# Graph network kernel: the feed-forward part, three normalisations and the projection to relations as one staggered stage

## What is computed

```python
# third layer, after the attention sums
att_out = out.mean(axis=1) + bias_att
x1 = layer_norm(att_out + h, ln1_g, ln1_b)
ff = relu(x1 @ W1 + b1) @ W2 + b2            # 64 -> 128 -> 64
x = x + layer_norm(ff + x1, ln2_g, ln2_b)
# fourth layer
h = maximum(_layernorm(x), 0)
out = h @ W_self.T + b_self
for r in range(3):
    msg = msg + where(edge_type == r, h[src] @ W_rel[r].T, 0)
out = relu(out.at[dst].add(msg))
x = x + out
```

## Time and profile before

| | us |
|---|---|
| median of 3 runs (9044.34 to 9046.91) | 9044.35 |
| the profiled execution, own time | 9047.62 |
| its span | 9045.9 |
| node stage: first transfer issued to last DVE instruction | 6677.37 to 6833.18 |
| relation stage: to the first instruction of the edge pass | 6833.48 to 6925.52 |
| edge pass: to the start of the last PE stage | 6925.52 to 8961.2 |

### The profile page before, as it was taken

How to read it: one execution, slowest core, us unless ns; L and a number is a source line. 1 busy time by engine, 2 the same in 40 slices (tenths; PEclk the granted TensorE clock), 3 DMA queues, 4 the chain that set the end, 5 groups by cost and what they waited for, 6 DMA issues and landing times. The chain is left out here.

```text
span 9045.9 us, 111398 instructions
## 1 busy us (share of the span) xinstructions
PE 4987.4 (55%) x30696; PEld 3834.2 (42%) x30696; DVE 5704.2 (63%) x16144; ACT 2155.6 (24%) x3911; POOL 6276.7 (69%) x5705
## 2 busy tenths in 40 slices
PE   5888888888569999356666666666672000000000
PEld 3554454444358787345555555555561000000000
DVE  6888888888679999466666666666663222222222
ACT  0111111111035555034444444444420000000000
POOL 4888888888645555467777777777513777777776
PEclk9888888888779999555555555555555555555555
DMA  3333333333311111123333333333311222222221
GB/s 84 35 35 35 35 37 35 35 35 35 48 42 23 22 23 21 39 51 56 57 57 56 56 57 57 57 56 57 74 51 39 53 53 52 49 53 53 53 53 48
DMA packets 635687, 421.21 MB, mean 47 GB/s; under 512 B 533255, under 2 KB 542756, under 8 KB 632784
## 3 DMA queue, kind: packets, MB, share of 16 engines
q0 software_dynamic: 322560, 216.89, 20.2%
q1 hardware_dynamic: 310766, 197.07, 7.4%
q10 hardware_dynamic: 2304, 6.55, 0.2%
HBM read 234.91 MB, written 185.18 MB: 46 GB/s over the span
## 5 line engine op out<-in xcount | busy, mean ns | idle before, releaser
L1791 POOL DMA_INDIRECT rows_l<-att_row_table,slots_l x2016 | 2003.1, 994 | 647.2 <-issue 613.8
L892 POOL DMA_INDIRECT acc<-val,idx x1240 | 1919.8, 1548 | 417.8 <-issue 373.1
L1003 POOL DMA_INDIRECT rows_l<-relation_table,idx x1612 | 1529.2, 949 | 578.6 <-issue 491.0
L1014 DVE SCALAR_TENSOR_TENSOR run<-run,mask,rows_l 128x64 f32<-128x64 f32 x1612 | 459.7, 285 | 1571.7 <-DMA rows_l<-relation_table,idx 1516.2
L701 PE MATMUL banks<-part 128*128 128x490 bf16 (+1 forms) x5580 | 1295.3, 391 | 0.0
L1050 PE MATMUL banks<-run,link 128*128 128x64 f32 x98 | 21.1, 421 | 2039.9 <-PEq L983 2039.9
L1905 PE MATMUL banks<-rows_l,prob 128*128 128x65 f32 x4032 | 920.2, 420 | 45.1 <-ACT piece_part L1841 41.5
L1905 PEld LDWEIGHTS banks<-rows_l,prob 128*128 128x128 f32 x4032 | 879.0, 330 | 106.0 <-issue 86.6
L1152 POOL DMA_INDIRECT gathered_rows<-h_table,gathered_index x600 | 577.9, 963 | 446.8 <-ACT gathered_index L1262 272.8
L1050 PEld LDWEIGHTS banks<-run,link 128*128 128x128 f32 x98 | 21.0, 333 | 2040.6 <-issue 2040.6
L701 PEld LDWEIGHTS banks<-part 128*128 128x128 bf16 x5580 | 582.9, 107 | 637.4 <-issue 151.1
(11 more groups left out here) (383 smaller groups left out, 9206.3 us busy)
## 6 DMA issues: line engine op xcount, KB each, us to landing
piece_sums<-kept_l SPq DMA_DIRECT2D x252, 264.0 KB, 4.3
running_sums<-run SPq DMA_DIRECT2D x62, 832.0 KB, 3.5
attr<-in_edge_attr SPq DMA_DIRECT2D x61, 624.0 KB, 3.7
rows_l<-att_row_table,slots_l POOLq DMA_INDIRECT x2016
rows_l<-relation_table,idx POOLq DMA_INDIRECT x1612, 2.5
acc<-val,idx POOLq DMA_INDIRECT x1240, 3.2
gathered_rows<-h_table,gathered_index POOLq DMA_INDIRECT x600
acc<-zero ACTq DMA_DIRECT2D x12, 512.0 KB, 16.7
```

The lines of the kernel that those rows point to most:

```text
L892: e.indirect_dma_start(acc_d[k], bass.IndirectOffsetOnAxis(ap=idx[h][:, r:r + 1], axis=0), val[h][:, r, :], None, compute_op=ALU.add).then ...
L1003: e.indirect_dma_start(gbuf[h][:, r, :], None, table, bass.IndirectOffsetOnAxis(ap=idx[h][:, r:r + 1], axis=0))\
L1791: e.indirect_dma_start(rows[u][:, r, :], None, hx_d, bass.IndirectOffsetOnAxis(ap=slots[u][:, r:r + 1], axis=0))\
```

## The change

The node stage and the relation stage become one Block written out by hand. All work is cut into the seven parts (`span(c)`, 128x448 each), and the parts are staggered: in round t (0 to 9) the first normalisation handles part t, the feed-forward part on PE part t - 1, the second normalisation part t - 2, and the third normalisation's end, the transposes of h and the relation matmuls part t - 3. Differences in the work itself:

- `res` is loaded by seven transfers, one per part, instead of one; then `w3` and `b3` on the same queue.
- The subtraction of the mean is one `scalar_tensor_tensor` with the sum and -1/D; squares are taken by ACT (`squares`), the root by ACT with scale 1/D and an epsilon tile as bias; gains and shifts are `tensor_tensor` on POOL. The copies to `step` are gone: PE transposes straight from `x1` and `hs`.
- The row sums are prepared in the attention tail: DVE adds the attention bias row to `hs`, be2 to `xs`, and be1 to `bf2`, so that the stage has no instructions for them. Those two whole-tensor additions stand behind `src_i` in the DVE list.
- Relation results: ACT copies both the 192 relation columns and the 64 own columns, two nodes at a time, from three rotating PSUM banks; stores are three per part (128x448 each), 21 in place of 42.
- `link`'s iota goes to POOL's list after its last gain. The comparison for `link` and the bias addition to `own` (128x3136) go to the head of the edge pass's DVE list (`first(e)`).

The diff, cut to its core:

```diff
-        def edge_pass(name, table, index, gbuf):
+        def edge_pass(name, table, index, gbuf, first):
...
                     e.memset(run[1][:, HALF - 1, :], 0.0).then_inc(s_step, 1)
+                    first(e)
...
                     e.scalar_tensor_tensor(src_i[:, :], typ[:, :], float(NP), src_i[:, :], ALU.mult, ALU.add)
+                    e.wait_ge(s_par, 16 * 9)
+                    every = [P, J, D]
+                    e.tensor_tensor(hs[:, :, :], hs[:, :, :], bc(vecs["batt"][:, :].unsqueeze(1), every), ALU.add)
+                    e.tensor_tensor(xs[:, :, :], xs[:, :, :], bc(vecs["be2"][:, :].unsqueeze(1), every), ALU.add)
+                    e.tensor_tensor(vecs["bf2"][:, :], vecs["bf2"][:, :], vecs["be1"][:, :], ALU.add)
...
+                @block.gpsimd
...
+                    def att_gain(c):
+                        e.wait_ge(s_c1, 3 * c + 3)
+                        e.tensor_tensor(scaled[:, span(c), :], res[:, span(c), :], row(vecs["g1"]), ALU.mult)\
+                         .then_inc(s_g1, 1)
+                    def shift(c):
+                        e.wait_ge(s_n1, c + 1)
+                        e.tensor_tensor(x1[:, span(c), :], scaled[:, span(c), :], row(vecs["be1"]), ALU.add)\
+                         .then_inc(s_x1, 1)
+                        e.wait_ge(s_q1, c + 1)
+                        e.tensor_tensor(res[:, span(c), :], scaled[:, span(c), :], row(vecs["bf2"]), ALU.add)\
+                         .then_inc(s_xb, 1)
...
+                    for t in range(NCH + 2):
+                        if t < NCH:
+                            att_gain(t)
+                        if t >= 2:
+                            ffn_gain(t - 2)
+                        if t < NCH:
+                            shift(t)
+                    e.iota(link[:, :, :], [[1, J], [J, P]], base=0, channel_multiplier=0,
+                           allow_small_or_imprecise_dtypes=True)
...
+                    def x_scale(c):
+                        e.wait_ge(s_r3, c + 1)
+                        e.reciprocal(var[:, 2, span(c)], var[:, 2, span(c)]).then_inc(s_v3, 1)
+                        e.wait_ge(s_v3, 2 * c + 2)
+                        e.scalar_tensor_tensor(hs[:, span(c), :], hs[:, span(c), :], 0.0, per(var, 2, c), ALU.max,
+                                               ALU.mult).then_inc(s_h, 1)
...
+                    for t in range(NCH + 3):
+                        if t < NCH:
+                            att_centre(t)
+                        if t >= 3:
+                            x_variance(t - 3)
+                        if 2 <= t < NCH + 2:
+                            ffn_centre(t - 2)
+                        if t >= 3:
+                            x_scale(t - 3)
+                        if t < NCH:
+                            att_variance(t)
+                        if 2 <= t < NCH + 2:
+                            ffn_variance(t - 2)
+                        if t < NCH:
+                            att_scale(t)
+                        if 2 <= t < NCH + 2:
+                            ffn_scale(t - 2)
...
+                    for t in range(NCH + 3):
+                        if t < NCH:
+                            square(s_c1, 3 * t + 3, res, 0, t, s_q1, s_v1, 1)
+                        if t >= 3:
+                            root(s_v3, 2 * (t - 3) + 1, 2, t - 3, s_r3)
+                        if 1 <= t < NCH + 1:
+                            copy_x1(t - 1)
+                        if 2 <= t < NCH + 2:
+                            square(s_c2, 3 * (t - 2) + 3, res, 1, t - 2, s_q2, s_v2, 0)
+                        if t < NCH:
+                            root(s_v1, 2 * t + 2, 0, t, s_r1)
+                        if 2 <= t < NCH + 2:
+                            root(s_v2, 2 * (t - 2) + 1, 1, t - 2, s_r2)
+                        if 1 <= t < NCH + 1:
+                            relu(t - 1)
+                        if t >= 3:
+                            copy_h(t - 3)
+                            relations_out(t - 3, 0)
+                            relations_out(t - 3, 1)
+                        if 2 <= t < NCH + 2:
+                            square(s_c3, 3 * (t - 2) + 3, hs, 2, t - 2, s_q3, s_v3, 0)
+                        if t >= 3:
+                            relations_out(t - 3, 2)
+                            relations_out(t - 3, 3)
...
+                    e.wait_ge(s_w3, 32)
+                    for t in range(1, NCH + 3):
+                        if t < NCH + 1:
+                            turn_x1(t - 1)
+                            up(t - 1)
+                            down(t - 1)
+                        if t >= 3:
+                            turn_h(t - 3)
+                            for k in range(NR):
+                                relate(t - 3, k)
...
+            def before_rows(e):
+                e.tensor_scalar(link[:, :, :], link[:, :, :], linkf[:, 0:1], None, ALU.is_equal)
+                e.tensor_tensor(own[:, :, :], own[:, :, :], bc(b3_s[:, :].unsqueeze(1), [P, J, D]), ALU.add)
+            edge_pass("l3", y3_d, src_i, g, before_rows)
```

More of the change, by code:

```diff
@@ L1429, in build @@
         quads.close()
[L1431 to L1441, removed]
         att = ExitStack()
@@ L2199, in _ @@
                         last.then_inc(s_proj, 1)
[L2201 to L2243, removed]
+        relating = ExitStack()
+        own = sb("own", [P, J, D], f32, relating)
+        link = sb("link", [P, J, P], f32, relating)
+        b3_s = sb("b3", [P, D], f32, relating)
         with ExitStack() as ctx:
             w3_s = sb("w3", [D, 4 * D], f32, ctx)
[L2246 to L2251, removed]
[L2252 to L2295 removed]
@@ new lines, in build @@
+            res = sb("att_out", [P, J, D], f32, ctx)
+            scaled = sb("normed", [P, J, D], f32, ctx)
+            x1 = sb("x1", [P, J, D], f32, ctx)
+            eps = sb("layer_eps", [P, 1], f32, ctx)
+            sq = [sb(f"squares{n}", [P, JB, D], f32, ctx) for n in range(3)]
+            mean = sb("node_sums", [P, 3, J], f32, ctx)
+            var = sb("node_squares", [P, 3, J], f32, ctx)
+            xt = sb("x1_t", [D, JB * P], f32, ctx)
+            hid = sb("hidden2_t", [P, JB * P], f32, ctx)
@@ new lines, in build @@
+            ht = sb("h3_t", [D, JB * P], f32, ctx)
+            rel = [sb(f"relations{k}", [P, 3, JB, D], f32, ctx) for k in range(2)]
+            NCH = J // JB
+            PARTS = [(0, 4), (4, JB)]
+            ROUNDS3 = [(j, min(j + 2, JB)) for j in range(0, JB, 2)]
+            NR = len(ROUNDS3)
+            s_res = [sem(f"nodes_att_loaded{c}") for c in range(NCH)]
+            s_rel = [sem(f"relations_stored{k}") for k in range(2)]
+            (s_c1, s_q1, s_g1, s_r1, s_n1, s_x1, s_xb, s_xt, s_xc, s_up, s_hid, s_down, s_c2, s_q2, s_g2, s_r2, s_n2,
+             s_c3, s_q3, s_r3, s_h, s_ht, s_hc, s_mul, s_ev, s_w3, s_v1, s_v2, s_v3) = (sem(f"nodes_{n}") for n in (
+                "att_centred", "att_squared", "att_gained", "att_root", "att_scaled", "x1", "x1_and_bias", "x1_turned",
+                "x1_t_copied", "hidden", "hidden_relu", "ffn", "ffn_centred", "ffn_squared", "ffn_gained", "ffn_root",
+                "ffn_added", "x_centred", "x_squared", "x_root", "h", "h_turned", "h_t_copied", "relations",
+                "relations_copied", "weights", "att_variance", "ffn_variance", "x_variance"))
@@ L2297, in build @@
         with ExitStack() as ctx:
             g = [sb(f"rows_l3_{h}", [P, HALF, D], f32, ctx) for h in range(2)]
-            edge_pass("l3", y3_d, src_i, g)
+            def before_rows(e):
+                e.tensor_scalar(link[:, :, :], link[:, :, :], linkf[:, 0:1], None, ALU.is_equal)
+                e.tensor_tensor(own[:, :, :], own[:, :, :], bc(b3_s[:, :].unsqueeze(1), [P, J, D]), ALU.add)
+            edge_pass("l3", y3_d, src_i, g, before_rows)
         with ExitStack() as ctx:
@@ L2309, in build @@
             stage(ch)
+        relating.close()
+        late.close()
+        att.close()
 def kernel(**inputs):
```

202 lines of the change are left out of this document (162 added, 40 removed).

## The result

| | before | changed |
|---|---|---|
| median of 4 runs | 9044.35 us (9041.55 to 9046.91) | 8933.02 us (8932.81 to 8935.93) |
| profiled execution | 9047.62 | 8935.93, span 8934.2 |

The ratio is 0.9878, with a 95% interval of 0.9861 to 0.9895. The forecast of 8932 is 1 us off, but some of its terms are off by more. From first transfer (6675.75) to the first instruction of the edge pass (6809.95) the stage takes 134.20 us, where 248.15 stood before. The edge pass from there to the end of the span takes 8934.2 - 6809.95 = 2124.25, against 9045.9 - 6925.52 = 2120.38.

A forecast was written before the change was run, and what follows sets the result against it. PE, at 16.4 us per part, was taken to bound the new stage: 8.6 + 16.6 + 86.0 + 20.0 + 4.2 = 135.4 against 248.15, with 0.5 lost in the edge pass, giving 8932 us; range 8914 to 8958.

The forecast's parts named there:

- The bound: New stage: PE has the most work per part, 16.4 us against 10.6, 8.4 and 5.2; PE-bound stage, chance 0.70.
- I add 0.3 for relus that come late: Rounds 3 to 7: 0.3 us added to each round's 16.4 for PE waiting on late relus.
- 0.45 for the copy: Rounds 3 to 7: stall of 0.4 to 0.5 us each, as ScalarE evacuates, squares, roots, then copies the transpose.
- PE's 16.4: PE's work per part: 8.3 us for a feed-forward turn plus 8.1 for a relation turn.
- The same step, round 3: First of rounds 3 to 7, which hold feed-forward and relations: all five priced at 17.2 us, 86.0 together.
- Rounds 1, 2, 8, 9, start and end: Stage outside full rounds: start 8.6 us, rounds 1 and 2 16.6, rounds 8 and 9 20.0, end 4.2.
- I take 0.5: Edge pass head: 0.5 us lost by gathers beside the moved VectorE work; 3.5 if GpSimd stood still for the whole comparison.
- the prediction's signs: Profile after: full rounds 17.2 us apart, PE's waits mostly for ScalarE's copy, under 1 a round; edge pass unchanged within 1.
- The additions moved into the attention tail: Attention bias and be2 additions behind `src_i`: cost 0, with 3.5 us of cover; 6.9 us were the cover gone.
- Hold-up: New stage: GpSimd and VectorE hold each other up, VectorE's round reaching 21 us; kernel 8954; chance 0.15.
- Clock: New rounds: TensorE's clock rises, PE's 16.4 falls to about 9, 37 us less; kernel 8895; chance 0.10.
- Parts that don't overlap: New stage: each part a serial chain of 40.6 us, stage 290.5, 42 slower; kernel 9086; chance 0.02.

The follow-up runs named there:

- first reordered kernel: Changed kernel with `link` comparison and `own` addition moved into the stage, ScalarE's round-3 copy, relu and some roots put earlier, function table loaded early: 8905.40 us, ratio 0.9867.

## Why the prediction was right, point by point

**The bound.** Right: full rounds are set by PE alone, at 16.04 for a forecast of 16.4. Doubling GpSimd's work, or giving it to VectorE, leaves them at 16.04; cutting PE's work is the one edit that shortens them.

**"I add 0.3 for relus that come late", and 0.45 for the copy.** Wrong in rounds 4 to 7: neither wait exists there. The 0.45 came from adding the last evacuation (0.5), the square (0.55) and the root (0.25) at their own lengths ahead of the copy, 1.3 us. In round 4 they take 6721.94 - 6720.95 = 0.99, since each starts before the one ahead of it has ended (the square at 6721.27 for 0.59 us, the root at 6721.75). The copy starts 1.09 after the transposes, where a turn of before has it at 1.07. PE's 16.4 was the sum of two turns, each read to the end of its last matmul; in the full rounds the next transposes start 0.21 and 0.07 before those ends (6728.90 against 6729.11, 6736.89 against 6736.96), and the two hand-overs through ScalarE's copies are 0.07 shorter each (1.72 for 1.79, 1.73 for 1.80), which makes it 16.04. Four rounds cost 64.25 for 68.8: 4.5 us too much in the forecast.

**The same step, round 3.** The sum was wrong the other way here: 19.67 for 17.2. It gave all five rounds one price. But in the first full round VectorE meets its full load of three normalisations without the lead that the relation matmuls of a round before give it later. Its two waits went when ScalarE's list was reordered (16.10).

**Rounds 1, 2, 8, 9, start and end.** Within 0.8 each. The start's 9.36 has the first VectorE operation 2.64 after the transfer's issue (2.1 forecast), and GpSimd's shift at 1.44, held up.

**"I take 0.5" for the edge pass.** Wrong by 3.4. Standing still for the whole comparison was the upper bound I worked out, and I let the sums' row (0.98 for 0.94) decide instead. But those sums take 0.3 us each, and what a gather waits for is the end of one instruction. That the length decides is my reading; no run varied it. I also gave that price to the comparison alone, and the addition costs as much. With it fell one of the prediction's signs, an edge pass unchanged within 1 us; another, full rounds 17.2 apart with short waits for ScalarE's copy, came out better, at 16.04 with no wait.

In the stage the errors are +0.8, -0.5, +2.5, -4.5, +0.6 and 0: -1.2. With +3.4 behind it and -1.6 ahead of it they make +0.6 on the profiled execution. That they all but cancel is luck; what holds is that none is above 5 us.

**The additions moved into the attention tail.** Cost 0, as forecast: they run from 6665.11 to 6671.86 beside PE and ScalarE, whose work in that stage ends later (ScalarE's last copy starts at 6671.96), and the stage begins at 6675.75.

**Rivals.** *Hold-up*: the mechanism is there (1.38 to 1.55 for 0.62), the time isn't in the full rounds, since PE's work hides it. GpSimd's 1.13 alone is under the 1.3 I took. The rule of the Trainium skill, page "SBUF — State Buffer", section "Who interferes with whom", that such a pair is shut out for a whole instruction, is borne out by these rows. *Clock*: it stayed at 0.50 (1.2 GHz) with PE busy 64.07 of 64.30 us. The rule of the Trainium skill, page "TensorE: Matmul & The Clock Gate", section "What's actually happening", that sustained activity releases the clock, is what the rival's 8895 stood beside; in this float32 stage the trace disagrees. *Parts that don't overlap*: run by itself this gives 29.4 us a part, not 40.6. GpSimd's gains and part of ScalarE's copies lie beside other work even then. It would still have been faster than before, since it decides from 34.5 on; this rival had its price wrong.

## What to carry to other kernels

Where two loops alternate between engines, cut the work in parts and stagger them until the engine with the most work per part never waits; then per-part loads of each engine forecast the time well. With lists in fixed order, look next at the first full round and at the last ones, where the cover is missing: what the busy engine needs belongs ahead of what a third engine feeds. Keep long VectorE instructions with SBUF operands away from the issue of GpSimd gathers, and put them where GpSimd has nothing on the path.

## What the runs showed of the hardware that I had not expected

- An addition of VectorE over 128 x 3136 with its operands in SBUF held one gather's issue at 2.75 instead of 0.97, as much as a comparison with a constant did (2.82). Gathers end 0.84 to 0.87 after the instruction that held them.
- VectorE operations on two SBUF tensors, 128x448, take 1.38 to 1.55 where they start beside a GpSimd gain or shift, but 0.62 beside GpSimd's iota, which only writes (first reordered kernel: iota from 6762.88 to 6768.49, such operations at 6764.54, 6765.20 and 6766.51, each 0.62). With one operand in PSUM they take 0.61 beside a gain.
- The kernel before took 9027.14, 9041.47 (one run), 9044.59 and 10302.20 on four chips; on the last the change gained 105 us, on the one before 110. On the last its edge pass takes 10201.1 - 7823.9 = 2377.2, some 250 more than on the one before, and the stage begins 1017 us later (7689.8 against 6672.9).
